# Cross-attention and FFN on one core: another set-up head, and k's second exponential ahead of x2's high part on ScalarE

## What is computed

```
x = x + xattn(layernorm(x), ctx)
  q = softmax over the 64 channels of a head of (Wq x) / 8 ; k = softmax over tokens of (Wk ctx) ; v = Wv ctx
  context = k v^T per head ; out = Wo (context^T q) + bo ; out = out / ||out|| * g * sqrt(128)
x = x + ffn(layernorm(x))
  w_int = [qweight & 15 ; (qweight >> 4) & 15]   (512 x 1024 packed, 1024 x 1024 unpacked)
  w = (w_int - round(zeros / scales)) * scales ; y = x w + bias
```

## Time and profile before

| | us |
|---|---|
| median of 3 runs | 705.52 |
| lowest and highest | 703.21, 708.35 |
| the profiled execution, its time | 706.99 |
| the profiled execution, its span | 704.9 |
| mean granted TensorE clock of that execution | 0.978 |

### The profile page before, as it was taken

How to read it: one execution, slowest core, us unless ns; L and a number is a source line. 1 busy time by engine, 2 the same in 40 slices (tenths; PEclk the granted TensorE clock), 3 DMA queues, 4 the chain that set the end, 5 groups by cost and what they waited for, 6 DMA issues and landing times.

```text
span 704.9 us, 11155 instructions
## 1 busy us (share of the span) xinstructions
PE 654.4 (93%) x3312; PEld 420.1 (60%) x3328; DVE 555.5 (79%) x900; ACT 449.6 (64%) x747; POOL 474.5 (67%) x406
## 2 busy tenths in 40 slices
PE   4858799999999999999999999999999999999987
PEld 3635556666666666656666666666666665666543
DVE  2997778888878788888878888888878887887844
ACT  3575666767585767667485666758575766748432
POOL 2166286776949496785949677694949678594820
PEclk9989889999999999999999999999999999999989
DMA  8125236363553637263454636255363724344451
GB/s 297 62 52 120 54 54 171 91 152 59 149 113 83 164 89 179 50 173 74 119 126 96 166 89 163 50 154 105 80 161 89 179 53 116 69 114 78 92 106 60
DMA packets 178871, 78.43 MB, mean 111 GB/s; under 512 B 168328, under 2 KB 169888, under 8 KB 178848
## 3 DMA queue, kind: packets, MB, share of 16 engines
q1 hardware_dynamic: 172512, 55.09, 36.9%
q10 hardware_dynamic: 6336, 23.07, 9.7%
HBM read 28.32 MB, written 8.39 MB: 52 GB/s over the span
## 4 chain that ended last, share of the span: by engine, by line
PE 34%; POOL 25%; issue 19%; DVE 12%; ACT 7%; DMA 1%; POOLq 0%; another core or an unknown queue 0%; DVEq 0%; ACTq 0%; SPq 0%
PE ps_m L1268 6%; POOL q_tok_lo L429 6%; POOL x L510 3%; POOL q_exp L419 3%; PE ps_m L1180 3%; POOL c_lo L473 3%; DVE q_sum L859 3%; POOL y L435 3%; PE ps_k L1110 3%; PE ps_o L1110 2%; POOL rn L492 2%; PE ps_k L1112 2%; PE ps_o L1111 2%; PE ps_k L1111 2%; PE ps_o L1112 2%
## 5 line engine op out<-in xcount | busy, mean ns | idle before, releaser
L429 POOL TENSOR_TENSOR q_tok_lo<-q_exp,q_tok_hi 128x1024 f16<-128x1024 f32 x64 | 140.0, 2189 | 85.8 <-ACT q_tok_hi L574 85.8
L419 POOL TENSOR_TENSOR q_exp<-q_exp,q_rec 128x1024 f32<-128x1024 f32 x64 | 122.2, 1910 | 5.0
L1180 PE MATMUL ps_m<-k_t,c_t 128*128 128x512 f32 x256 | 119.8, 602 | 0.0
L563 ACT ACTIVATE q_exp<-q_exp 128x512 f32<-128x512 f32 x128 | 80.5, 629 | 45.9 <-DVE q_exp L852 45.9
L840 DVE TENSOR_REDUCE k_nmax<-ps_k 128x1 f32<-128x1024 f32 x64 | 78.1, 1220 | 40.1 <-PE ps_k L1112 40.0
L558 ACT ACTIVATE k_exp<-ps_k,k_nmax 128x1024 f32<-128x1024 f32 x64 | 71.1, 1110 | 55.1 <-DVE k_nmax L840 55.1
L574 ACT ACTIVATE q_tok_hi<-q_exp 128x1024 f16<-128x1024 f32 x64 | 67.6, 1056 | 49.8 <-POOL q_exp L419 49.8
L847 DVE TENSOR_REDUCE q_nmax<-ps_q 128x8 f32<-128x512 f32 x128 | 87.3, 682 | 11.2 <-PE ps_q L1112 9.6
L852 DVE TENSOR_TENSOR q_exp<-ps_q,q_nmax 128x512 f32<-128x512 f32 x128 | 88.5, 692 | 5.1 <-DVE q_nmax L847 0.2
L1110 PE MATMUL ps_q<-wq_hi,xn_lo 128*128 128x512 f32 x128 | 74.4, 581 | 9.7 <-DVE q_exp L852 7.0
L417 POOL TENSOR_TENSOR q_rec<-q_rec,q_range 128x16 f32<-128x16 f32 x64 | 15.6, 244 | 93.3 <-DVE q_rec L862 93.3
(11 more groups left out here) (185 smaller groups left out, 1385.1 us busy)
## 6 DMA issues: line engine op xcount, KB each, us to landing
x_res<-in_x ACTq DMA_DIRECT2D x16, 512.0 KB, 3.4
out_x<-y SPq DMA_DIRECT2D x15, 512.0 KB, 2.9
x_in<-in_x ACTq DMA_DIRECT2D x14, 512.0 KB, 4.7
c_in<-in_ctx ACTq DMA_DIRECT2D x14, 512.0 KB, 6.0
x_in<-in_x SPq DMA_DIRECT2D x2, 512.0 KB, 6.0
c_in<-in_ctx SPq DMA_DIRECT2D x2, 512.0 KB, 8.1
q_hi<-q_tok_hi SPq DMA_TRANSPOSE x64, 3.1
q_lo<-q_tok_lo SPq DMA_TRANSPOSE x64, 3.1
```

The costliest lines, as they stand in the source:

```text
L419: nc.gpsimd.tensor_tensor(pair, pair, rec.unsqueeze(2).to_broadcast([P, 2 * HEADS, DH]), ALU.mult).then_inc(qs_done, 1)
L429: nc.gpsimd.tensor_tensor(q_tok_lo[p % 2][:], q_exp[:, 2 * p:2 * p + 2, :].rearrange("p t d -> p (t d)"), q_tok_hi[p % 2][:], ALU.subtract ...
L563: nc.scalar.activation(q_exp[:, j, :], q_exp[:, j, :], ACT.Exp).then_inc(qexp_done, 1)
L1180: last = nc.tensor.matmul(ps_m[:], c_t[s][:, t, :], k_t[:, t, :], start=(t == 0), stop=(t == TC - 1))
```

## The change

It has two parts.

**The head.** In iteration -1 DVE goes by an order of its own: x's statistics first, c's maximum, xn, the weights' low parts, the rows' arithmetic (taken out of iteration 0), c's top, k's first maximum. POOL does the power of x's variance and c_lo at the start of the iteration, ACT rounds xn before it copies wo_t, and PE does `project_k(0, 0)` ahead of `transpose_c(1)`. The columns, the 24 transposes and the six copies of the rows are gone: scales are spread by one DMA into scale_bc, and the three bf16 parts of -round(zeros/scales) and bias/scales are split on the 8 x 2 x 128 rows (two ACT, two POOL instructions) and laid into ffn_rows by 12 small DMAs of SP. vo is copied by ACT instead of DVE. The eight picks and conversions are spread over two iterations: picks in steps 1, 3, 5, 6 of iteration 0 and 1, 2, 3, 5 of iteration 1, conversions in steps 2, 4, 6, 7 and 2, 3, 4, 6. Mixing and splitting on the full width in iteration 1 are gone.

**The loop.** On ACT `exp_k(a, s, 1)` stands directly behind `exp_q(0)`, ahead of `high_x2` and `high_q(c, 3)`; this holds in every iteration from 0 to 15. gs_undo becomes a tensor_scalar with gs_col as its scalar operand.

```diff
@@ SP, before the iterations
+            sp.dma_start(scale_bc[:], scales.rearrange("o a -> (a o)").partition_broadcast(P)).then_inc(scale_spread, 16)
+            sp.wait_ge(consts_made, 10)
+            for part in range(3):
+                sp.wait_ge(rows_split, (1, 3, 4)[part])
+                for r in range(4):
+                    row = 32 * part + r
+                    sp.dma_start(ffn_rows[row:row + 1, :].rearrange("a (t c) -> a t c", t=TC),
+                                 row_parts[:, r // 3, part, :]).then_inc(rows_placed, 16)
@@ POOL
+                if first:
+                    fit_x()
+                    low_c()
...
+                if isinstance(i, int) and i == 0:
+                    both = rows_in[:, 1:3, :]
+                    pool.wait_ge(rows_split, 1)
+                    nc.gpsimd.tensor_tensor(both, both, row_parts[:, :, 0, :], ALU.subtract).then_inc(rows_split, 1)
+                    pool.wait_ge(rows_split, 3)
+                    nc.gpsimd.tensor_tensor(row_parts[:, :, 2, :], both, row_parts[:, :, 1, :],
+                                            ALU.subtract).then_inc(rows_split, 1)
@@ ACT
-                    if j == 4 and isinstance(i, int) and i == FIRST:
+                    if j == 4 and first:
+                        high_x()
                         set_up_rest()
...
                     if do_a:
                         exp_q(j)
+                    if j == 0 and do_a:
+                        exp_k(a, s, 1)
                     if j == 0 and do_f:
                         high_x2()
                     if j == 0 and do_c:
...
-                    if j < 3 and do_a:
+                    if 1 <= j < 3 and do_a:
                         exp_k(a, s, j + 1)
...
-                    if isinstance(i, int) and i == 0:
-                        set_up_ffn(j)
-                    if isinstance(i, int) and i == 1 and j == 2:
-                        act.wait_ge(rows_mixed, 2)
-                        nc.scalar.activation(ffn_rows[:], zero_bc[:], ACT.Copy).then_inc(rows_split, 1)
+                    if isinstance(i, int) and i == 0 and j == 0:
+                        move_vo()
                         act.wait_ge(rows_split, 2)
-                        nc.scalar.activation(ffn_rows[32:64, :], bias_bc[32:64, :], ACT.Copy)
-                        nc.scalar.activation(ffn_rows[64:96, :], bias_bc[64:96, :], ACT.Copy).then_inc(rows_split, 1)
+                        nc.scalar.activation(row_parts[:, :, 1, :], rows_in[:, 1:3, :], ACT.Copy).then_inc(rows_split, 1)
+                    if isinstance(i, int) and i == 0 and j in (2, 4, 6, 7):
+                        convert_nibble((2, 4, 6, 7).index(j))
                     if isinstance(i, int) and i == 1 and j == 0:
-                        convert_nibble(2 * RC - 1)
-                        act.wait_ge(w_converted, 2 * RC)
                         nc.scalar.dma_start(x_res[:], x[c]).then_inc(xres_loaded, 16)
+                    if isinstance(i, int) and i == 1 and j in (2, 3, 4, 6):
+                        convert_nibble(4 + (2, 3, 4, 6).index(j))
@@ DVE
-                    nc.vector.tensor_tensor(gs_undo[:], g_undo[:], gs_col[:], ALU.mult).then_inc(fit_steps, 1)
+                    nc.vector.tensor_scalar(gs_undo[:], g_undo[:], gs_col[:], None, ALU.mult).then_inc(fit_steps, 1)
...
+                if isinstance(i, int) and i == FIRST:
+                    stats_x()
+                    mean_x()
+                    abs_c()
+                    norm_x()
+                    set_up()
                     set_up_rows()
+                    top_c()
+                    max_k(n, 0)
+                    return
...
                     if isinstance(i, int) and i == 0:
-                        set_up_late(j)
-                    if isinstance(i, int) and i == 1 and j == 1:
-                        set_up_mix()
-                    if isinstance(i, int) and i == 1 and j in (3, 5):
-                        set_up_split((j - 3) // 2)
+                        if j == 1:
+                            set_up_gains()
+                        elif j == 3:
+                            set_up_top()
+                        if j in (1, 3, 5, 6):
+                            pick_nibble((1, 3, 5, 6).index(j))
+                    if isinstance(i, int) and i == 1 and j in (1, 2, 3, 5):
+                        pick_nibble(4 + (1, 2, 3, 5).index(j))
@@ PE
-                            set_up_cols()
-                        elif j < 4:
-                            set_up_row(2 * (j - 1))
-                            set_up_row(2 * (j - 1) + 1)
...
+                    if j == 7 and do_n and isinstance(i, int) and i == FIRST:
+                        project_k(n, 0)
                     if j == 7 and do_n:
                         transpose_c(1)
```

More of the change, by code:

```diff
@@ L286, in loads @@
             return 8 * (b - s) + 16
+        NIBBLES = [(m + 2 * late, high) for late in range(2) for high in range(2) for m in range(2)]
         FIRST, LAST = -1, NB + 2
@@ L403, in _ @@
             nc.gpsimd.memset(rs_parts[:], 0.0).then_inc(consts_made, 1)
-            pool.wait_ge(consts_made, 7)
+            nc.gpsimd.memset(ffn_rows[:], 0.0).then_inc(consts_made, 1)
+            pool.wait_ge(consts_made, 8)
             nc.gpsimd.memset(rs_parts[:, 0:3, 3], 1.0).then_inc(consts_made, 1)
@@ L470, in iteration @@
                         low_q(a, 0)
[L471 to L474, removed]
+                    if j == 3 and do_n and not first:
+                        low_c()
                     if j == 4 and do_a:
@@ L482, in iteration @@
                         add_y(1)
[L483 to L488, removed]
+                    if j == 6 and do_n and not first:
+                        fit_x()
                     if j == 6 and do_c:
@@ L523, in set_up, with move_vo @@
                 nc.scalar.activation(wq_hi[:], ps_q[:], ACT.Copy).then_inc(whi_done, 1)
+            def move_vo():
+                act.wait_ge(vo_ready, 1)
+                for q in range(2):
+                    nc.scalar.activation(vo[:].rearrange("p (k q o) -> p q k o", q=2, o=P)[:, q],
+                                         ps_o[q][:].rearrange("p (k o) -> p k o", k=HC), ACT.Copy).then_inc(vo_moved, 1)
             def set_up_rest():
@@ L559, in exp_k, with high_x @@
                                          accum_out=k_sum[:, sums, j:j + 1]).then_inc(kexp_done, 1)
+                first = isinstance(i, int) and i == FIRST
+                def high_x():
+                    act.wait_ge(xn_done, n + 1)
+                    if begun(8 * a):
+                        act.wait_ge(q_ready, 8 * a)
+                    nc.scalar.activation(xn_hi[1 - s][:], xn[:], ACT.Copy).then_inc(xnhi_done, 1)
                 def exp_q(j):
@@ L739, in iteration @@
                         exp_k(n, 1 - s, 0)
-                    if j == 6 and do_n:
-                        act.wait_ge(xn_done, n + 1)
-                        if begun(8 * a):
-                            act.wait_ge(q_ready, 8 * a)
-                        nc.scalar.activation(xn_hi[1 - s][:], xn[:], ACT.Copy).then_inc(xnhi_done, 1)
+                    if j == 6 and do_n and not first:
+                        high_x()
                     if j == 7 and isinstance(i, int) and i == END:
@@ L1391, in iteration @@
                         mix_m(4, 5)
-                    if j == 7 and do_n:
+                    if j == 7 and do_n and not (isinstance(i, int) and i == FIRST):
                         project_k(n, 0)
```

177 lines of the change are left out of this document (73 added, 104 removed).

## The result

The changed kernel takes **710.07 us** (median of 5, 709.28 to 711.78) against 705.52 us (also of five executions, not of the three that the table above names); the ratio is 1.0068, with a 95% interval of 1.0035 to 1.0101. So it is slower by 0.7%, less than the 1% that I had set as the bound. The profiled execution is the median one: 710.07 us, span 708.2. The spans differ by 708.2 - 704.9 = +3.3 us, where the prediction had +4.5.

A forecast was written before the change was run, and what follows sets the result against it. Two regimes: PE bounds the loop, other engines' orders and waits set the head's pace. Loop +15.0 and head -10.5 make +4.5 on the median 705.5, so 710 us; range 699 to 719, forecast case 702 to 716.

The forecast's parts named there:

- The loop chain: Loop: 6.57 us from k_nmax's end to spread_rs; +0.79 per even, +1.4 per odd iteration, +15.0 us in sum.
- Whether a later stage swallows it: Loop: PE, busy 97.8%, has no pause to absorb 0.8 to 1.4 us, so the delay is paid each time.
- The head: Start to m_t of iteration 1 -6.1, iteration 1 -4.4, together -10.5 us; bounds -4 and -16.
- The start: Iterations -1 and 0: with xn_lo early, k's exponentials gain between 0 and 2.34 us; taken as 0.75.
- gs_undo: Iteration 0: as a tensor_scalar it takes 2.0 us off DVE's path; in the loop worth nothing.
- The picks: Iteration 0: -2.7 and -3.3, fourth pick +1.4; iteration 1: two picks at 0.69, each waiting 0.7 for POOL.
- Rival 2: Head: every DVE pick caught behind POOL, 2.18 instead of 0.69 us; head gives -4 to -5, 716 us; chance 0.13.
- Iteration 1: Head, iteration 1: -1.5 + 1.0 - 1.3 - 1.3 - 0.7 - 0.6 = -4.4 us.
- clock term: Iteration 1: mix_g took 1.85 us at half clock; fewer PE pauses keep the clock: -1.3 with the projection behind.
- Rival 1: Loop: the move pays, x2n_lo not holding shift_q(1) up; eight times 0.63 is -5.0, 690 us; chance 0.17.
- Rival 3: Loop: the clock falls with PE's pauses; 2 us at half clock in fourteen iterations, +14, 724 us; chance 0.05.
- rival 4: Loop at its lower and head at its upper bound cancel: 702 us, inside the forecast's case of chance 0.65.

The follow-up runs named there:

- Experiment 3: The changed kernel with x2n_lo on DVE behind shift_q(1) instead of ahead of it: 699.81 us, ratio 0.9919.
- experiment 10: The changed kernel with DVE's loop written out iteration by iteration: 705.06 us, ratio 0.9997.
- Experiment 9: The kernel of experiment 1 with iteration -1 in its old order on all engines: 695.63 us, ratio 0.9855.
- experiment 8: The kernel of experiment 1 with all eight picks and conversions in iteration 0 again, none in iteration 1: 697.04 us, ratio 0.9904.
- experiment 1: The changed kernel with k's second exponential back behind x2n_hi and q_tok_hi(c, 3), so the new head alone: 695.28 us, ratio 0.9855.
- experiment 6: The kernel before with only gs_undo as a tensor_scalar: 703.89 us, ratio 0.9987.
- experiment 2: The kernel before with only k's second exponential moved ahead of x2n_hi: 720.84 us, ratio 1.0213.
- experiment 5: The changed kernel with an unread full-width copy of vo on ACT between the exponential and x2n_hi, iterations 2 to 15: 729.84 us, ratio 1.0340.
- experiment 4: The changed kernel with the exponential one place later on ACT, between x2n_hi and q_tok_hi(c, 3): 689.26 us, ratio 0.9767.
- experiment 7: The kernel of experiment 4 with DVE's loop written out iteration by iteration: 686.37 us, ratio 0.9731.

## Why the prediction was right, and where it was not

**What bounds the kernel.** The two regimes hold. The head was set by the other engines' orders: -10.2 us from the head alone. The loop is PE's: in iteration 9 its listed waits grew from 0.75 to 1.87 us and the iteration from 40.13 to 41.66. The other 0.4 us of growth are in no wait that the trace lists; they are booked as PE's busy time.

**The loop chain.** Right in mechanism and length (6.61 against 6.57 us). Counted from m_t, spread_rs came 0.82 us later in iteration 10 (put at 0.79) and 1.43 in iteration 9 (put at 1.39). PE's wait for k_t ahead of `transpose_k`, 0.29 us, was not foreseen; it adds nothing to the sum, since PE waits for the end of the same chain after it. The even iterations from 4 to 14 rose by 0.85 us in the mean, put at 0.79; the odd ones from 5 to 13 by 1.58, put at 1.39 and entered as 1.4. The whole is +16.5 in the trace, put at +15.0 with an upper bound of 18. The order alone measured +15.0 by the medians, but that is no proof of the term: in its trace too the loop is +16.5 and the tail -1.5, and the agreement of the two 15.0 is luck. Of the surplus in the trace 0.9 us is the odd iterations', 0.4 the even ones' and 0.2 that of iterations 2, 3 and 15 (1.50, 1.11 and 0.94 us, put at 1.1 each). Experiment 3 shows x2n_lo as the largest link, and experiment 10 shows why the odd ones are the worse: the turn of DVE's loop delays k_nmax in each odd iteration by some 0.7 us, and the new order pays it. In the old order the wait was there as well (0.75 us in iteration 9), and its odd iterations were no longer than the even ones, which had the 0.63 us at ps_k instead. The prediction gave the odd ones their own, larger sum from the earlier trace rows but didn't name the loop's turn.

**Whether a later stage swallows it.** Right: iterations 3 to 15 all rose, by 0.8 to 1.6 us.

**The head.** The sum was right (-10.5; -11.8 in the trace, -10.2 by the medians), its terms less so:

- *The start*, put at 0.75, is not settled. The second k_nmax of the head came 2.1 us earlier in the trace. DVE before, then after:

```profile
23.71 1.23 DVE L840 TENSOR_REDUCE k_nmax<-ps_k 128x1 f32<-128x1024 f32 x1 [1.14 <-PE ps_k L1112]
```

```profile
21.58 1.23 DVE L846 TENSOR_REDUCE k_nmax<-ps_k 128x1 f32<-128x1024 f32 x1 [0.98 <-PE ps_k L1127]
```

  Both show a k_nmax that waits for PE. Before, project_q(0) waited for xn_lo and project_k(0, 1) came behind it in PE's queue, its matmuls 0.43 us apart; after, they are 0.23 apart. Experiment 9's trace shows the old start 2.1 us later again (23.21 against 21.07 us), its medians none of it. A single execution is a weak witness here: experiment 8, with the same iteration -1 as experiment 1, has this k_nmax at 19.98.
- *gs_undo*, put at -2.0 in iteration 0, was booked in the wrong place: alone it gains 0.06 us there (experiment 6), 1.7 us in iteration 1 and loses 1.3 of these in iteration 2, in one trace; its medians give 0.9 us in all. The term failed in taking a delayed DVE instruction for a delayed path.
- *The picks.* By the spread I had won 2.7 and 3.3 in iteration 0. It does win there, 4.0 us (experiment 8), but pays as much in iteration 1 by the trace. Three of the eight picks met POOL; the view by source, in the changed kernel:

```profile
L836 DVE TENSOR_SCALAR y<-og x2: 637/661/685, 28.1 to 44.3; 128x1024 int32<-128x1024 int32 x2
L836 DVE TENSOR_SCALAR nibble<-sq x2: 682/1536/2391, 35.2 to 48.8; 128x1024 int32<-128x1024 int32 x2
L836 DVE TENSOR_SCALAR y<-spare x2: 684/684/685, 65.2 to 73.8; 128x1024 int32<-128x1024 int32 x2
L836 DVE TENSOR_SCALAR nibble<-x x2: 1831/2168/2504, 69.6 to 82.9; 128x1024 int32<-128x1024 int32 x2
```

  2.39, 1.83 and 2.50 us against 0.68 for the rest. I had put the fourth at +1.4 (it cost 1.7) and two of iteration 1 at +0.7 each (they cost 1.1 and 1.8). Rival 2, with all five caught, overstated it.
- *Iteration 1*, put at -4.4, is -3.6. Of its terms, high_q behind the exponential was booked at +1.0 and measures nothing: under the new head the iteration takes 40.32 us with it and 40.37 without (experiment 1). The clock term held: mix_g took 1.09 us instead of the 1.85 of the earlier trace rows. The other terms were not measured apart.

The errors of the head are of both signs and cancel; the sum is better than its parts, which is luck in part.

**The tail**, put at nothing, is 1.5 us shorter (37.02 to 35.55 us). It goes with the new order more often than not, but isn't tied to it. The five kernels with the exponential ahead of x2n_hi have 35.55 (the changed one), 35.56, 35.68, 35.76 and 36.34 (experiments 2, 3, 5, 10); those with it behind q_tok_hi 37.02 (before), 36.88, 37.05, 35.84 and 37.05 (experiments 1, 6, 8, 9); those between 36.63 and 35.79 (experiments 4, 7). Before and after, mix_out of the last batch starts 5.26 us after the m_t of iteration 16 with its matmuls 0.43 us apart, at a granted clock of 0.50. PE about 5 us further on, before, then after (mix_out starts at 673.14 and 677.91):

```profile
678.21 0.63 PE L1110 MATMUL ps_o<-q_hi,g_lo 128*128 128x512 f16 x1
```

```profile
682.63 0.38 PE L1125 MATMUL ps_o<-q_hi,g_lo 128*128 128x512 f16 x1
```

Before, the matmuls close up (0.22 us apart) only at 679.1, 5.9 us after mix_out's start; after, at 680.8, after 2.9 us. Three microseconds more at full clock in place of half are the 1.5 us. In experiment 8, with the old order, they close up 3.6 us after mix_out's start; in experiment 10, with the new, after 4.2. Why the clock recovers sooner in one kernel than in another stays open; no run changed the tail alone.

**The rivals.** Rival 1 is refuted for the place that the change chose and borne out one place later (experiment 4). Rival 3 is refuted for this kernel and seen in experiment 5. Rival 2 falls with the head's -10.2, rival 4 with the loop, which cost more than the lower bound that it needs.

**The rule weighed.** The five picks of the changed kernel that took 0.64 to 0.69 us ran while POOL ran nothing; the three slow ones each started inside a POOL instruction on the full width and ended 0.5 to 0.6 us behind its end. The first of them, the timeline of POOL and DVE:

```profile
48.42 2.23 POOL L423 TENSOR_TENSOR q_exp<-q_exp,q_rec 128x1024 f32<-128x1024 f32 x1
48.80 2.39 DVE L836 TENSOR_SCALAR nibble<-sq 128x1024 int32<-128x1024 int32 x1
```

POOL's ends at 50.65, the pick at 51.19. This fits what the prediction took from the Trainium skill, "SBUF — State Buffer", section "Who interferes with whom": the two exclude each other for a whole instruction, and so a pick pays only when a POOL instruction is running. The rows fit that section in a further point: the same product of two columns takes 1143 ns in the median (621 to 2135) as an instruction with two tensors in SBUF, and 213 to 215 ns, sixteen times out of sixteen, with one of them given as the scalar. The page says that a DVE instruction with at most one SBUF input, outside the two-port modes, doesn't contend with GpSimd; the trace agrees, taking the scalar form to be such an instruction, which no view shows.

## What to carry to other kernels

When an instruction is moved ahead on an engine that executes in order, list what it passes, and follow the consumer of each passed item into its own engine's queue: here the exponential won PE 0.63 us in every second iteration and delayed, by way of x2n_hi and x2n_lo, a q chunk that had nothing to do with either, for a net loss of 15 us. Move it only past what nobody is waiting for: the same edit one place later won 6 us over the head alone. And price a stall by what is late next and not by its length: taking 0.6 us off the wait at g_lo was worth 0.74 us in the odd iterations of one kernel and 0.18 in those of another.

## What the runs showed of the hardware

- Half clock can come after short waits of PE alone, none over 1.24 us: with PE busy 6.49 of 9 us, the next 8 us ran at 0.79 (experiment 5, in seven of fourteen iterations, for about 1.1 us each); the same loop without the copy, with about a microsecond less of waits an iteration, stayed at 1.00.
- The turn of DVE's loop, once in each pass of two iterations, delayed DVE's k_nmax by 0.66 us in experiment 10's iteration 9, and PE's wait for g_lo by 0.6 (0.74 to 0.15 in experiment 7, 0.76 to 0.16 in experiment 10).
- A pick that met POOL took 1.83 to 2.50 us instead of 0.64 to 0.69 and ended 0.5 to 0.6 us behind POOL's instruction.
- Early in the kernel the printed clock can mislead. Busy time from 19 to 23 us in experiment 9, then in experiment 1:

```profile
19.00:23.00 4.00, 4.00 (x9) 2.77 (x9) 2.60 (x8) 1.61 (x4) 0.67 (x1) 1.00 0.43 142
```

```profile
19.00:23.00 4.00, 3.64 (x28) 2.90 (x29) 2.31 (x3) 1.91 (x5) 0.68 (x1) 1.00 0.78 265
```

  Both print 1.00, but the matmuls of project_k(0, 1) stand 0.43 us apart in the first and 0.23 in the second. In the kernel before the same matmuls also stand 0.43 us apart, and there the column says 0.59 from 20 to 22 us and 0.55 from 22 to 24. So in experiment 9 the distance between matmuls tells the rate and the column doesn't.
